# Attention with tiles of a feed-forward layer on one core: which PSUM bank each transpose goes to, which engine empties one of them, and when x is transposed and loaded

## What is computed

```python
q, k, v = einsum('bsx,xMnd->Mbnsd', x, qkv)            # 16 heads of 64
a = einsum('bnsd,bntd->bnst', q, k) * 64 ** -0.5
bias = where(rel >= 0, cum[:, clip(rel, 0)], -30000.0) # by distance, causal
a = softmax(a + bias)
x = layernorm(x + einsum('bnsd,ndx->bsx', a @ v, out_w))
# feed-forward: xr, xk mix each token with the one before it
out = sigmoid(xr @ W_r.T) * (square(relu(xk @ W_k.T)) @ W_v.T)
x = layernorm(x + out)
```

## Time and profile before

| | |
|---|---|
| median of 3 runs | 1105.91 us (1104.41 to 1106.25) |
| the profiled execution | 1106.52 us, its span 1104.8 us |
| TensorE busy | 1061.2 us, 96% of the span |
| ScalarE busy | 781.5 us, 71% |
| VectorE busy | 757.6 us, 69% |
| GpSimd busy | 226.3 us, 20% |
| mean granted TensorE clock | 0.99 of full speed |
| DMA | 145.08 MB, mean 131 GB/s |

### The profile page before, as it was taken

One profiled execution on the slowest core, in us unless ns is written; L12 is line 12 of the kernel. 1 busy time (PEld: TensorE's weight loads), 2 busy tenths in 40 slices (PEclk: granted clock), 3 DMA queues, 4 the chain that ended last, 5 costly groups with the idle time before them and its releaser, 6 DMA issues. The chain is left out here.

```text
span 1104.8 us, 21923 instructions
## 1 busy us (share of the span) xinstructions
PE 1061.2 (96%) x6983; PEld 752.1 (68%) x6983; DVE 757.6 (69%) x1983; ACT 781.5 (71%) x2002; POOL 226.3 (20%) x227
## 2 busy tenths in 40 slices
PE   7999999999999999999999999999999999999995
PEld 4675666666666777676777676677666677667774
DVE  5665556566666777776777776767776777776766
ACT  4876677776766787777777776777777678777743
POOL 1121112222111222221222221122221122221110
PEclk9999999999999999999999999999999999999997
DMA  3545454554545455655454654555654554564610
GB/s 97 147 116 146 132 141 110 134 137 124 149 115 143 126 138 129 151 137 145 126 147 119 149 148 121 132 145 131 155 139 127 133 139 121 145 151 117 210 55 21
DMA packets 104400, 145.08 MB, mean 131 GB/s; under 512 B 11328, under 2 KB 70608, under 8 KB 104288
## 3 DMA queue, kind: packets, MB, share of 16 engines
q1 hardware_dynamic: 101728, 142.57, 49.7%
q10 hardware_dynamic: 2560, 1.12, 0.4%
HBM read 58.41 MB, written 20.22 MB: 71 GB/s over the span
## 5 line engine op out<-in xcount | busy, mean ns | idle before, releaser
L791 DVE CUSTOM_DVE_ANT_0 prob<-ps_rows,table 128x128 f32<-128x128 f32 (+7 forms) x512 | 379.7, 750 | 84.8 <-PE ps_rows L1122 72.7
L589 ACT ACTIVATE prob<-prob,low 128x128 f32<-128x128 f32 (+7 forms) x512 | 394.7, 773 | 39.9 <-DVE low L791 35.8
L1122 PE MATMUL ps_rows<-stacks 128*128 128x512 f32 (+3 forms) x1536 | 392.9, 367 | 3.9 <-DMA stacks<-k_lo 3.1
L1139 PE MATMUL ps_t<-ident_r,prob_r 128*128 128x128 f32 x1984 | 283.6, 262 | 7.6 <-ACT pt L607 3.7
L1139 PEld LDWEIGHTS ps_t<-ident_r,prob_r 128*128 128x128 f32 x1984 | 212.0, 141 | 89.2 <-issue 72.4
L1163 PE MATMUL ps_o<-pt,v_pair 128*64 128x512 f32 (+3 forms) x1536 | 269.5, 493 | 0.0
L809 DVE COPY pt<-ps_t 128x512 f32<-128x512 f32 (+3 forms) x288 | 165.1, 582 | 144.4 <-PE ps_t L1139 144.0
L1122 PEld LDWEIGHTS ps_rows<-stacks 128*128 128x128 f32 x1536 | 244.6, 189 | 22.6 <-DMA stacks<-k_lo 4.1
L498 POOL TENSOR_TENSOR mix_sb<-mix_sb,inv_all 128x512 f32<-128x512 f32 x64 | 82.3, 1286 | 790.3 <-PE ps_rows L1122 605.4
L1163 PEld LDWEIGHTS ps_o<-pt,v_pair 128*64 128x64 f32 x1536 | 102.0, 137 | 176.7 <-issue 164.5
L607 ACT ACTIVATE pt<-ps_t 128x512 f32<-128x512 f32 (+3 forms) x384 | 175.3, 457 | 25.2 <-PE ps_t L1139 24.3
(11 more groups left out here) (133 smaller groups left out, 787.2 us busy)
## 6 DMA issues: line engine op xcount, KB each, us to landing
inv_all<-inverse_sums SPq DMA_DIRECT2D x128, 128.0 KB, 3.4
stacks<-q_hi SPq DMA_DIRECT2D x62, 256.0 KB, 3.8
stacks<-q_lo SPq DMA_DIRECT2D x62, 256.0 KB, 4.1
stacks<-k_hi SPq DMA_DIRECT2D x62, 256.0 KB, 3.9
stacks<-k_lo SPq DMA_DIRECT2D x62, 256.0 KB, 4.8
mix_transposed<-mix_sb SPq DMA_DIRECT2D x62, 256.0 KB, 2.0
table<-bias_by_distance SPq DMA_DIRECT2D x64, 192.0 KB, 3.6
mix_tile<-mix_transposed SPq DMA_DIRECT2D x24, 448.0 KB, 3.8
```

The source lines that it names most:

```text
L589: nc.scalar.activation(row, row, ACT.Exp, bias=low[:, r:r + 1], scale=-1.0, accum_out=total[:, r:r + 1]).then_inc(s_exp, 1)
L791: nc.vector.tensor_tensor_reduce(prob[:, r % PSLOTS, 0:width], ps_rows[:, score_at(r):score_at(r) + width], table[n % 2][:, h, 0:width][:, ...
L1122: ins = nc.tensor.matmul(ps_rows[:, at + c0:at + c1], q_st(h, n)[:, P * i:P * i + P], k_st(h, n, low_part)[:, c0:c1], start=(low_part == 0 ...
L1139: ins = nc.tensor.transpose(t_bank[TBANK[k]][:, P * b:P * b + P].bitcast(F32R), prob_r[:, r % PSLOTS, at:at + P], ident_r[:, :])
```

## The change

- `TBANK`: bank 9 goes to ps_o (before: ps_t1), bank 19 to ps_t0 (before: ps_o), bank 20 to ps_o (before: ps_t0), bank 22 to ps_t0 (before: ps_o), bank 23 to ps_o (before: ps_t1). ps_o has four banks in place of three. Banks 9 and 16, the first behind a mix, wait for that mix's copy.
- `EVACUATOR`: bank 22 is copied out by DVE (before: ACT).
- `INV_READY`: the second half of the sums is inverted in slot 12 (before: 13).
- `X_SLOTS`: x of a later batch is transposed in slots 8 and 13 (before: 0 and 13). x of batch 1 is loaded at the program's start.
- SP issues `spread_inverse(n, 0)` behind `stack_k` (before: ahead of it).
- x_cur is loaded in halves: the front half once the fifth of the six projections has read it (slot 10), the back half behind slot 15 as before.

```diff
--- before.py
+++ after.py
@@ -60,8 +60,9 @@
 BANKS = bank_list()
 NBANKS = len(BANKS)
 
-EVACUATOR = "010111010100011001110111"
-TBANK = [k % 2 for k in range(16)] + [2, 0, 1, 2, 0, 1, 2, 1]
+EVACUATOR = "010111010100011001110101"
+TBANK = [0, 1] * 4 + [0, 2] + [0, 1] * 3 + [2, 0, 1, 0, 2, 1, 0, 2]
+BEHIND_MIX = (9, 16)
 
 
 def evacuated(engine, k):
@@ -87,9 +88,9 @@
 MIX_FAR = (2, 5)
 MIX_NEAR = 11
 TILE_LAG = PAIRS + 1
-X_SLOTS = (0, 13)
+X_SLOTS = (8, 13)
 CH = 13
-INV_READY = (4, 13)
+INV_READY = (4, 12)
 INV_BANK = (5, 21)
 
 
@@ -207,6 +208,7 @@
         s_mu = sem("mu_ready")
         s_w = [sem(f"pair_weights_loaded{a}") for a in range(2)]
         s_x = sem("x_transposed_loaded")
+        s_x_front = sem("x_transposed_front_loaded")
         s_x_first = sem("x_transposed_first_half")
         s_proj = sem("projected")
         s_hi = sem("hi_ready")
@@ -347,11 +349,11 @@
             sp.wait_ge(s_seq_dram, 16)
             sp.wait_ge(s_zero, 2)
             load_table(0)
+            sp.dma_start(x_later[:, :, :], x_tiles[:, TILES:2 * TILES, :]).then_inc(s_x_later, 16)
 
             def load_x_later(b):
 
-                if b > 1:
-                    sp.wait_ge(s_x_mm, 2 * (b - 1))
+                sp.wait_ge(s_x_mm, 2 * (b - 1))
                 sp.dma_start(x_later[:, :, :], x_tiles[:, TILES * b:TILES * b + TILES, :]).then_inc(s_x_later, 16)
 
             def store_x_transposed(b):
@@ -364,12 +366,17 @@
                 sp.wait_ge(s_proj, NPROJ * (m - 1))
                 sp.dma_start(w_cur[m % 2][:, :, :], qkv_pairs[m % PAIRS, :, :, :]).then_inc(s_w[m % 2], 16)
 
-            def load_x_transposed(b):
-
-                sp.wait_ge(s_proj, NPROJ * PAIRS * b)
+            def load_x_front(b):
+
+                sp.wait_ge(s_proj, NPROJ * PAIRS * b - 1)
                 if b == 1:
                     sp.wait_ge(s_xt_dram, 16 * (BATCH - 1))
-                sp.dma_start(x_cur[:, :], xt_d[b, :, :]).then_inc(s_x, 16)
+                sp.dma_start(x_cur[:, 0:SEQ // 2], xt_d[b, :, 0:SEQ // 2]).then_inc(s_x_front, 16)
+
+            def load_x_back(b):
+
+                sp.wait_ge(s_proj, NPROJ * PAIRS * b)
+                sp.dma_start(x_cur[:, SEQ // 2:], xt_d[b, :, SEQ // 2:]).then_inc(s_x, 16)
 
             def store_mix(n, g):
 
@@ -443,22 +450,26 @@
                 store_inverse(n, 0)
                 if prev:
                     store_mix(n - 1, 1)
-                spread_inverse(n, 0)
+                if not more:
+                    spread_inverse(n, 0)
                 if following >= 0 and following % TILES == 0:
                     tile_loads(following, slice(PAIRS - 1, PAIRS))
                 if more:
                     sp.wait_ge(s_lo, 4 * n + 8)
                     stack_k(sp, n + 1, 0, s_stack[0])
+                    spread_inverse(n, 0)
                 if not more:
                     load_mix_last(PAIRS - 2, PAIRS - 1)
-                if n + 1 in range(1, BATCH):
+                if n + 1 in range(2, BATCH):
                     load_x_later(n + 1)
+                if (n + 2) % PAIRS == 0 and n + 2 < PAIR_STEPS:
+                    load_x_front((n + 2) // PAIRS)
                 store_mix(n, 0) if more else None
                 if n in range(1, BATCH):
                     store_x_transposed(n)
                 store_inverse(n, 1)
                 if (n + 2) % PAIRS == 0 and n + 2 < PAIR_STEPS:
-                    load_x_transposed((n + 2) // PAIRS)
+                    load_x_back((n + 2) // PAIRS)
                 if tile_too:
                     tile_store(n - TILE_LAG)
 
@@ -1083,6 +1094,9 @@
                     pe.wait_ge(s_xt, 2 * (m - 2) + done)
                 if c == 0 or m == 0:
                     pe.wait_ge(s_w[m % 2], 16 * (m // 2) + 16)
+                    if m >= PAIRS:
+                        pe.wait_ge(s_x_front, 16 * (m // PAIRS))
+                if c == 1:
                     pe.wait_ge(s_x, 16 * (m // PAIRS) + 16)
                 if m > 0:
                     wait_chunk(m, c - 1)
@@ -1129,8 +1143,8 @@
                 for k in (k for k in range(NBANKS) if BANKS[k][0] == r):
                     _, b0, nb = BANKS[k]
 
-                    if TBANK[k] == 2 and 2 not in TBANK[:k]:
-                        pe.wait_ge(s_raw, 2 * n + 2)
+                    if k in BEHIND_MIX:
+                        pe.wait_ge(s_raw, 2 * n + 1 + BEHIND_MIX.index(k))
                     else:
                         engine, count = emptied(n, k)
                         pe.wait_ge(s_ev[engine], count)
@@ -1154,6 +1168,8 @@
                     pe.wait_ge(s_v, 2 * n + 2)
                     for which in range(2):
                         last_bank = max(k for k in range(NBANKS) if ROWS[BANKS[k][0]][1] < GROUP * (g + 1))
+                        if g == 0:
+                            last_bank = BEHIND_MIX[0]
                         pe.wait_ge(s_ev[which], EVACUATED[which] * (n + 1) + evacuated(which, last_bank))
                     pe.wait_ge(s_raw, 2 * n + g + 1)
                 final = GROUP * (g + 1) - 1
```

## The result

The changed kernel takes 1092.64 us, the median of 4 runs (1090.87 to 1093.89), beside 1105.7 for the kernel before: a ratio of 0.9882, with an interval of 0.9865 to 0.9899. That is 13 us faster. The forecast was 1084.5 (21 us faster): the direction is right, the time lies within the range of 1077 to 1094, and over a third of the gain is missing. The forecast's own band ended at about 1090; the range reached to 1094 for two rivals, and neither of them happened as it was told, so that the time lies in the range is in part luck.

A forecast was written before the change was run, and what follows sets the result against it. TensorE, busy 1061.2 of 1104.8 us, and what makes it wait were taken as the bound. The terms summed to 21.9 us off the profiled 1106.5, giving 1084.6, put at 1084.5 with a range of 1077 to 1094.

The forecast's parts named there:

- The banks in tile steps: Pair steps 9 to 30: bank 19's 0.34 and bank 9's 0.25 us losses go, 0.50 kept each step, 11.0 us.
- The queue: SP issues keys ahead of the spreading: 1.4 plus 1.2 us gained early; inverse sums some 3 us later cost nothing.
- Pair step 0's keys and the low clock: End of pair step 0: the 1.41 us wait for keys goes (1.4), and the 1.2 GHz stretch behind it (1.2).
- x of later batches: Slot 0's waits go (4.5 us) and a low-clock stretch (1.3); slot 8's new wait for ps_m costs 2.7.
- x_cur in halves: Start of pair step 7 and later batches: waits for x_cur of 1.69 and some 0.2 go, 1.9 us.
- Bank 0's new wait: Starts of pair steps 1 to 8: bank 0 waits some 0.25 us for VectorE's copy of bank 22.
- 0.44 + 0.22: Pair steps without a tile: 0.34 at bank 19 plus 0.1 of bank 9's; at starts, 0.47 - 0.25 at banks 1 and 0.
- the gains are swallowed: Rival: ScalarE's chain behind slot 11 or a VectorE copy leaves tile steps gaining 0.15, not 0.50; 1092 us, chance 0.18.
- The low clock did not return in slot 8: Rival: slot 8's 1.1 us wait in pair steps 1 to 3 brings 1.2 GHz back; 1089.6 us, chance 0.12.

The follow-up runs named there:

- e10: The kernel before with bank 9 alone moved to ps_o, with the waits for the mix's copy that go with it: 1102.01 us, ratio 0.9977.
- e7: The changed kernel with VectorE's sum and statistics in slot 13 instead of 12, behind its 256-wide row: 1082.1 us, ratio 0.9793.
- e1: The changed kernel with the spreading of the inverse sums ahead of the keys again in SP's queue: 1087.57 us, ratio 0.984.
- e6: The kernel before with the changed queue order alone, the loads of inv_all behind the keys: 1106.22 us, ratio 1.0012.
- e11: e1 with GpSimd multiplying the near half of the mix twice in pair steps 9 to 30: 1106.62 us.
- e2: The changed kernel with the spreading right behind the store of the inverse sums, ahead of the mix's store and the keys: 1102.51 us, ratio 0.9986.
- e3: The kernel before with the bank tables, bank 22's copy by VectorE and the inversion in slot 12 alone: 1094.18 us, ratio 0.9908.
- e5: The kernel before with x_cur loaded in halves alone: 1104.4 us, ratio 0.9998.
- e4: The kernel before with x of later batches in slots 8 and 13 and batch 1's loaded early, alone: 1101.85 us, ratio 0.9984.

## Why the prediction was partly right

- **The banks in tile steps: size off.** I took 0.50 of 0.59 as kept (all of 0.34 and half of 0.25 are 0.46; the 0.50 was rounded up), because ScalarE's chain behind slot 11 would eat half of *bank 9's* gain. The runs show that most of bank 9's gets through (0.20 of 0.33, e10; the 0.25 that I had read was too small) and that most of *bank 19's* does not (0.11 of 0.34): the next waiting place lay behind it, at the tile's first product. I had followed TensorE's banks over that boundary ("bank 0 finds its buffer empty") but not the tile's own buffer, ps_m, whose last reader is ScalarE's copy of v. 21 x 0.19 = 4.0 us. e7 returns all of it, and the 0.27 at this place with it (2.28 against 2.02).
- **The queue: the step that failed.** "POOL needs them only when the mix is copied: nothing". The sums do land about when the mix is copied, but not always before: GpSimd then starts up to 2.7 us later (3.44 behind the mix copy in place of 0.73), and what I costed at nothing is what GpSimd runs into, VectorE's sum. About 6 us of tile steps in the changed kernel (e1) and 4.5 in that of before (e6), against 1.2 to 2.65 us gained in pair step 1. e11 shows the cause without the queue. In pair step 0 the keys did come sooner, as forecast; it is the word "nothing" that failed. The Trainium skill, page "SBUF — State Buffer", section "Who interferes with whom", says that a VectorE instruction with two inputs in SBUF contends with a GpSimd instruction that reads SBUF, and that whichever starts first holds the shared ports for its whole length. The traces agree: in all stretched sums of the changed kernel, e6, e7 and e11 GpSimd had started first and the sum ended 0.15 us behind it (less than its own 0.28, so it had not stood still from its start to GpSimd's end, or its start is counted early; the traces do not tell which), and VectorE's copies out of PSUM beside the same multiply kept their 0.64 us (488.55, 493.48). Had I asked of this page what the later multiply would stand beside, a rival of 22 x up to 0.9 us would have been in the prediction.
- **Pair step 0's keys and the low clock: right, the clock in part by luck.** 2.6 forecast, 2.65 (e6). Their wait is gone and the window at full clock. But the low clock is not in every execution: the same wait was 1.38 to 1.53 us in e2, e3 and e5 and 1.2 GHz followed, and 1.22 to 1.28 in e1, e4, e10 and e11, where it did not. Against those the queue is worth the wait alone, 1.2 (pair step 1 in e1).
- **x of later batches: right in kind, its size not settled.** 4.5 + 1.3 - 2.7 = 3.1 forecast; the profile of e4 has 4.7 over pair steps 1 to 4, 3.9 without the clock of pair step 1, with slot 8's waits at 2.0; the medians say about 2.
- **x_cur in halves: right in the profile (1.92 for 1.9), not shown by time.** A half of 256 KB lands in 3.3 us (changed kernel) and 3.7 (e5), where all 512 KB took 3.7. The Trainium skill's fixed cost ("DMA: Bandwidth & Descriptors", "Anatomy of one DMA — SWDGE (gpsimd) path") gave 2.9 as an estimate; the trace agrees that halving the bytes does not halve the time, and goes further. Both loads stayed covered.
- **Bank 0's new wait: right.** 0.25 forecast; eight waits of 0.29 or 0.30 at the starts of pair steps 1 to 8. Pair steps 4 to 6 gained 0.57 each for 0.44 + 0.22; of bank 9's gain I had kept 0.1, but in pair step 6 TensorE gains 0.3 at bank 9 and loses 0.3 again at bank 10, where the waits of 0.20 stand. (The five starts at which bank 1 had waited 0.47 are those of pair steps 4 to 8, not "5 to 9".)
- **Rivals.** The time came near that of "the gains are swallowed" (1092). That is mostly luck: its mechanism (a ScalarE chain sets TensorE's next start) was at work at another place and cost 4.0 of the 22 x 0.35 = 7.7, and the larger loss came by one that none of the rivals had. The low clock did not return in slot 8; TensorE's waits there were 0.7 us.

The sum: 21.9 forecast; 4.0 lost to the copy of v, 5.7 to longer tile steps, and, by difference, the other terms together 2 us above the forecast, of which 1.3 lie ahead of the first mix copy, a stretch that varies from 40.9 to 42.5 us between the kernels. That is 14.2 of the 14.4 us between the two profiled spans.

What stays open: why GpSimd's start in the changed kernel varies from 0.73 to 3.44 us behind the mix copy from step to step. The landing of the spreading decides it. In pair steps 16 and 24, where the load of mix_tile stands ahead, the second of its two loads is issued 1.1 and 1.5 us ahead of the mix copy in place of 2.9 to 3.0. In 11, 12, 17, 18, 22, 23, 25 and 29 it is issued as early as elsewhere and lands up to 1.3 us later than in pair step 14; what delays that landing was not isolated.

## What to carry to other kernels

Before calling a later arrival free, look at which engine starts later by it, and at what every other engine does in the new place: one engine can hold another up without a semaphore, and the profile shows it only as an instruction that is longer than its kind. When a stall is removed, follow every buffer that the waiting engine needs next, across the boundary into the next step, and follow it back to the other engine's queue; moving one short job behind the one that is waited for (e7) was worth 10 us, about half of it by the wait at the tile's product and half by fewer stretched steps. And where a wait for a transfer stands in a queue, its cost is that of everything that has to be issued behind it (e2).

## What the hardware showed

- VectorE's sum of two SBUF tiles of 128x128 takes 0.28 us alone, and up to 1.39 beside GpSimd's multiply of SBUF tiles that started first; the multiply keeps its 1.29. Started behind the sum (pair step 24), the multiply leaves it its 0.28. No run here has GpSimd start while the sum is under way.
- The low clock does not follow from the length of a wait alone. Waits of 1.24 and 1.69 were not followed by it, one of 1.21 (e5) was, and in e10 one of 1.36 for x_cur:

```profile
243.78 1.94 PE L1096 MATMUL ps_m<-x_cur,w_cur 128*128 128x512 f32 x2 [1.36 <-issue]
```

```profile
243.80:247.60 3.80, 3.80 (x8) 1.02 (x10) 0.69 (x1) 1.19 (x3) 0.00 (x0) 0.55 0.59 166
```

  Each such stretch cost its pair step 1.3 to 1.4 us, which is what I had taken for one.
- The 12 runs of e5, whose profile has three low-clock stretches (two as in the earlier trace rows, and the one above), lie between 1100.38 and 1107.27 us; the 4 of the changed kernel, which has no wait over 0.8 us between the first scores and the last part, lie within 3 us, but e11's 12, with a wait of 1.22, lie within 3.6. That such waits make the time scatter fits this and is not shown.
